# Delta stage of a fused decoder layer: squares for the gate's statistics in two halves, half of the sums after the copy of the states, and another order of two copies of the inverse

## The reference, cut to what matters

```python
q, k, v = silu(conv(x @ Wq)), silu(conv(x @ Wk)), silu(conv(x @ Wv)); beta = sigmoid(x @ Wb)
# delta rule by chunks, per head (4 heads of 64)
attn = where(strict, -(kb @ k.T), 0); T = inv(eye - attn); u = T @ v; w = T @ kb      # kb = k * beta
step: u_i = u0 - w_i @ S; o_i = q_i @ S + local @ u_i; S = S + k_i.T @ u_i
paths = stack([fir_s(v), fir_m(v), fir_l(v), o_delta, v])                             # 5 paths
stats = for each path and head: mean(t), mean(t*t), mean(|t|), sqrt(sum(t*t))
logits = gelu(concat(x, stats) @ gW1 + gb1) @ gW2 + gb2
probs = softmax(logits / tau) * (1 - sum(eps)) + eps
y = rmsnorm(sum_p probs_p * path_p) * norm_w @ Wo
```

## Time and profile before

| | us |
|---|---|
| median of 3 runs | 940.93 (940.04 to 941.74) |
| the profiled execution, its own time | 938.07 |
| its span in the profile | 936.2 |
| steps 1 to 9 of the delta stage in it | some 183 to 400 |

### The profile page before, as it was taken

One profiled execution on the slowest core, in us unless ns is written; L12 is line 12 of the kernel. 1 busy time (PEld: TensorE's weight loads), 2 busy tenths in 40 slices (PEclk: granted clock), 3 DMA queues, 4 the chain that ended last, 5 costly groups with the idle time before them and its releaser, 6 DMA issues.

```text
span 936.2 us, 17146 instructions
## 1 busy us (share of the span) xinstructions
PE 822.1 (88%) x6187; PEld 613.2 (65%) x6187; DVE 594.9 (64%) x1431; ACT 448.9 (48%) x831; POOL 350.7 (37%) x321
## 2 busy tenths in 40 slices
PE   6888879789988998898478898899979999999895
PEld 5676657667766666677345555556866777777774
DVE  5799979656888888877546677853552333333255
ACT  5677747455655665443046665565412322223221
POOL 9421210003455645632202246334531332222684
PEclk9899989878999999799678999999999999999998
DMA  5689849988959875546635455308031222221512
GB/s 176 198 241 299 248 127 253 341 198 189 250 178 247 255 215 148 171 137 219 225 131 170 159 184 179 127 25 268 26 98 41 63 68 57 70 57 46 157 63 68
DMA packets 160723, 149.18 MB, mean 159 GB/s; under 512 B 92289, under 2 KB 129217, under 8 KB 159361
## 3 DMA queue, kind: packets, MB, share of 16 engines
q1 hardware_dynamic: 157232, 138.72, 50.3%
q0 software_dynamic: 3408, 9.38, 2.7%
HBM read 86.90 MB, written 61.03 MB: 158 GB/s over the span
## 4 chain that ended last, share of the span: by engine, by line
PE 56%; DVE 12%; ACT 12%; POOL 8%; DMA 5%; issue 5%; SPq 1%; POOLq 0%; DVEq 0%; ACTq 0%
PE ps L2730 10%; PE ps L2745 5%; PE ps L665 4%; PE ps L2594 3%; PE ps L1397 3%; DMA queries<-q_pad 3%; POOL hank L344 2%; PE ps L422 2%; POOL kept L2877 2%; DVE big L1449 2%; PE ps L2607 2%; PE ps L2103 2%; PE ps L2216 2%; PE ps L1552 2%; PE ps L1405 2%
## 5 line engine op out<-in xcount | busy, mean ns | idle before, releaser
L2730 PE MATMUL ps<-wr,xbT 128*128 x312 | 100.6, 465 | 1.8 <-ACT xbT L2766 1.8
L2153 DVE TENSOR_REDUCE cmx<-ps 128x4 f32<-128x1024 f32 x64 | 77.4, 1219 | 37.6 <-PE ps L2103 36.0
L2192 ACT ACTIVATE cross_room<-ps 128x1024 f32<-128x1024 f32 x64 | 65.6, 1024 | 52.1 <-PE ps L2116 50.5
L2819 POOL DMA_INDIRECT y_dram<-yb,dest_row x39 | 37.3, 957 | 134.2 <-DVE dest_row L2795 129.7
L1365 POOL TENSOR_TENSOR st<-st,exponent 128x20 f32<-128x20 f32 x16 | 56.5, 3532 | 64.4 <-DVE st L1340 62.8
L2730 PEld LDWEIGHTS ps<-wr,xbT 128*128 128x128 f32 x312 | 59.4, 191 | 30.1 <-issue 3.5
L549 DVE SCALAR_TENSOR_TENSOR room<-room 128x256 f32<-128x256 f32 x144 | 58.3, 478 | 11.1 <-ACT room L498 11.1
L2804 DVE TENSOR_TENSOR cross_room<-cross_room,ps 128x352 f32<-128x352 f32 x39 | 20.3, 521 | 60.6 <-PE ps L2730 60.6
L2774 ACT ACTIVATE cross_room<-ps 128x352 f32<-128x352 f32 x39 | 18.1, 465 | 73.6 <-PE ps L2730 73.6
L2810 DVE TENSOR_SCALAR yb<-ps,weight 128x256 f32<-128x256 f32 x39 | 18.9, 484 | 50.8 <-PE ps L2745 50.8
L422 PE MATMUL ps<-room,weights 128*128 128x256 f32 x192 | 46.2, 392 | 3.6 <-DMA room<-in_conv_v 2.6
(11 more groups left out here) (355 smaller groups left out, 2210.3 us busy)
## 6 DMA issues: line engine op xcount, KB each, us to landing
xs_dram<-staged SPq DMA_DIRECT2D x17, 1040.0 KB, 6.5
room<-in_gW SPq DMA_DIRECT2D x8, 1280.0 KB, 8.2
tok_dram<-room SPq DMA_DIRECT2D x8, 768.0 KB, 7.1
fir_dram<-room SPq DMA_DIRECT2D x6, 1024.0 KB, 7.3
paths<-fir_dram SPq DMA_DIRECT2D x48, 128.0 KB, 3.6
keys<-k_pad SPq DMA_DIRECT2D x28, 196.0 KB
queries<-q_pad SPq DMA_DIRECT2D x28, 196.0 KB
xb<-xs_dram SPq DMA_DIRECT2D x39, 130.0 KB, 2.3
```

The costliest lines, as they stand in the source:

```text
L2153: V.tensor_reduce(mx[:, :, half, :, g].rearrange("p t c -> p c t"), ps[:, pair(h), :].rearrange("p c (t k) -> p c t k", t=TT), AX.X, ALU.m ...
L2192: S.activation(pT[g % 2][:, pair(h)].rearrange("p c k t -> p (c k t)"), ps[:, pair(1 - h), :].rearrange("p c n -> p (c n)"), ACT.Exp, scal ...
L2730: m = nc.tensor.matmul(ps[:, 2 * (j % 2) + half, 0:FF], xbT[j % 2][:, k, :], wr[:, bass.ds(e, 1), k, half, :].rearrange("p e n -> p (e n)" ...
L2819: G.indirect_dma_start(env.y2_dram, bass.IndirectOffsetOnAxis(ap=dest_row[:, j % NI:j % NI + 1], axis=0), yb[j % 4][:], None).then_inc(*y_ ...
```

## The change

The squares (ACT) are made by two instructions, one for each half of the tokens: the first in round 1, the second in round 2 behind the copy of u. Each waits only until the sums of the batch before have read its half. DVE sums the squares of half 0 in round 2 and moves the other three sums a round on: those of half 1 stand in round 3 behind the copy of the states, |t| of half 0 in round 4, |t| of half 1 in round 5, behind lT and ahead of the last five softmax steps. In the inverse, the last two copies (L1189) change places: the one out of PSUM bank 0 comes first, and PE's turn of k, which writes bank 0, waits for one copy fewer. The sums, the copies and their sizes are the same.

```diff
         def pe_invert(b):
...
-            pe.wait_ge(s.gw, 4 * b)
+            pe.wait_ge(s.gw, 4 * b - 1)
             turned(0, tok[i][:, :, 1]).then_inc(*s.k_turned.up())
...
         def dve_invert(b):
...
-            for h, bank in enumerate((3, 0)):
+            for h, bank in ((1, 0), (0, 3)):
...
         def act_statistics(b):
...
-            act.wait_ge(s.stat, 6 * (b - 1) + 3)
-            S.activation(sqs[:].rearrange("p n t d -> p (n t d)"), paths[i][:].rearrange("p n t d -> p (n t d)"),
-                         ACT.Square).then_inc(*s.sq.up())
-            yield
+            for t in range(TT):
+                act.wait_ge(s.stat, 6 * (b - 1) + 2 + t)
+                S.activation(sqs[:, :, t], paths[i][:, :, t], ACT.Square).then_inc(*s.sq.up())
+                yield
...
         def dve_statistics(b):
...
             stat(0, 0, paths[i])
             yield
-            dve.wait_ge(s.sq, b + 1)
+            dve.wait_ge(s.sq, 2 * b + 1)
             stat(1, 0, sqs)
+            yield
+            dve.wait_ge(s.sq, 2 * b + 2)
             stat(1, 1, sqs)
             stat(0, 1, paths[i])
             yield
             stat(2, 0, paths[i], apply_absolute_value=True)
             yield
             stat(2, 1, paths[i], apply_absolute_value=True)
             yield
```

## The result

| | before | after |
|---|---|---|
| median of the runs, us | 940.51 (10 runs, 932.17 to 945.38) | 947.11 (10 runs, 942.9 to 951.15) |
| ratio, 95% interval | | 1.0068 (1.004 to 1.0096) |
| the profiled execution, own time / span | 938.07 / 936.2 | 946.84 / 945.0 |

The change makes the kernel 0.68% slower, some 6.4 us. Lines of the gate have moved by two in the changed kernel (the products L1449 are L1451, L1493 is L1495, L1580 is L1582, POOL's sum L1510 is L1512) and the squares L1332 are L1333; L1053, L1183, L1189, L1313 and L1340 are the same.

What follows compares the result with a forecast made beforehand. Full steps were taken as bound by a ring of waits through DVE, ACT and PE. Steps 1 and 2 -4.0, step 3 +2.0, steps 4 to 7 +7.8, step 9 +1.5: +7.3 on 940.93, 948.2 us; range 939.8 to 951.5.

Steps and rivals of the forecast that it cites:

- rival (b): DVE and POOL taking turns costs only the nearest row's 0.7 us; steps 3 to 7 pay 1.1 each; 943.9 us; chance 0.14.
- (d): Faster: DVE wins the port for its three products in a row, steps 3 to 7; -5.0, 935.9 us; chance 0.16.
- (f): Square between the gelus needs two more ACT table loads of 1.28 us in steps 4 to 7; 958.5 us; chance 0.01.
- Rival (e): The later softmax alone costs time, DVE-POOL turns and clock unchanged; -0.5, 940.4 us; chance 0.12.
- Step 2, -4.0: Steps 1 and 2: earlier copy of the states and one copy fewer before k gain 4.0 us, bounds 3.0 and 4.2.
- The cap: Step 3 cannot turn k before its tokens land at 220.1, so at most 4.2 us are gained.
- Step 3, +2.0: Gate of step 3: softmax ends later and all of POOL's work meets DVE's products, +2.0 us.
- rival (c): PE's longer waits drop its clock to 1.2 GHz for 2 to 4 us in steps 5 to 7; +3, 951; chance 0.08.
- Full steps, 4 x 1.95: Steps 4 to 7 each lose 1.9 us on DVE and POOL plus 0.05 on ACT, +7.8 together.
- The order: Full steps: moved sum of \|t\| ends the softmax 1.48 us later, idle before L1183 covers part; +0.35 a step.
- the lock: Full steps: DVE's and POOL's products take turns on the shared port, whole instructions at a time; +1.55 us a step.
- the ring: Steps 5 to 8: the chain of waits through DVE, ACT and PE, holding the squares (2.23 us) but no sums.

Runs made afterwards that it cites:

- e6: The changed kernel, unchanged, profiled a second time; 941.89 us (one run).
- e8: The changed kernel with the last two copies of the inverse back in the old order; 945.13 us, ratio 1.0067 to the kernel before.
- e1: The changed kernel with batches 1 to 7 back to whole squares and old sum places, swap kept; 935.14 us, ratio 0.9964 to the kernel before.
- e7: The changed kernel with only the sum of squares of half 1 behind the copy of the states, softmax at its old place; 937.31 us, ratio 0.9964.
- e2: The changed kernel with batch 0 (step 2) as in the kernel before, swap kept; 949.2 us, ratio 1.0094 to the kernel before.
- e3: The kernel before with only the swap of the inverse's last two copies; 939.26 us, ratio 0.9955, resting on 7 of 12 runs.
- e9: The kernel before with SP issuing the next tokens and inverses ahead of the paths in steps 1 and 2; 944.46 us, ratio 1.0023.
- e12: The kernel before with only the squares made in halves, sums at their old places, no swap; 941.49 us, ratio 0.9971.
- e5: The kernel before, unchanged, profiled a second time; 934.33 us (one run).
- e4: The changed kernel with POOL's two products waiting for DVE's three; 945.39 us, ratio 1.0083 to the kernel before.
- e11: e7 with SP issuing the next tokens and inverses ahead of the paths in steps 1 and 2; 940.02 us, ratio 0.9963 to the kernel before.

## Why the prediction was right, and which terms were off

The direction, the place and the mechanism were right: forecast 948.2 us (+7.3), measured 947.11 beside 940.51 (+6.6), within the range. That the two numbers are so close is in part luck: the full steps lost 4.8 us and not 7.8, nearer to the 1.1 a step of rival (b) than to the 1.95 of the forecast, and by the profiles the start of cross moved by 4.4 and 6.1 us; what is missing up to 6.6 lies where single profiles scatter by several us. Rivals (d) and (f) fell: DVE lost its turn to POOL three times in every full step, and the second square ran between the gelus with no table load (L1333 at 309.90, L1428 at 311.07). Rival (e) fell with the products of 4.01.

- **Step 2, -4.0:** the mechanism was right, L1213 stands behind L1075 and the copy of the states comes 3.7 us sooner counted from the turn of k, as forecast. The swap gives 0.33 at each of two turns instead of 0.41. The gain to k in step 3 was 4.4 in the first pair of profiles, and 1.9 in the second, in which step 2 took 22.5 us before and 20.9 after. The cap is real, its place at 220.1 was lucky (220.22 in e6, but 219.06 in e8, 221.25 in e1, 223.55 in e7). Wrong was the clause that the change doesn't move SP: L1023 was issued at 211.03 in the first profile, 1.7 sooner, and anywhere up to 216.26 (e7) in the others, and it landed after 7.1 to 7.9 us, in e8 after 5.6. In the first profile and in e8 the cap was not reached.
- **Step 3, +2.0:** measured +2.3 and +3.3, but for another reason in part. The products went from 2.58 to 3.86, +1.3; the rest is the lower clock at the start of the step, +1.2 and +2.0 by the turns. Kernels with the old order in step 2 had it too (e2, e3, e9 and e12, above), so it isn't shown to be the change's. Over all profiles this stretch is 1.4 longer with the new order in step 3 than with the old one (27.3 against 25.9, six and eight profiles): the term was put at 2.0 and is some 1.4.
- **The clock in full steps (rival c):** it did fall now and then, ahead of step 5 in the changed kernel (0.50 at 272 to 276 us) but also in e5 (0.57), and ahead of step 6 in e6 (0.50 at 300 to 304), with a turn 0.4 to 0.6 longer; in e7 the turn was 1.3 longer, in e3 3.1, and in e8 three turns together 3.5. So the size that rival (c) gave, +3, occurs in single executions, with the old order of the sums (e3) as with the new (e8); that the change makes it more frequent isn't shown. In e3 and e7 it began with the tokens: in step 7 PE waited 2.22 and 1.83 us for them ahead of the turn of k, as it did for 0.6 to 1.2 us in e1, e4, e5, e11 and e12. So the cap that the forecast had in step 3 is near in full steps as well. The turn in e3:

```profile
335.46 1.11 PE L1053 MATMUL ps<-ident,kept 128*128 128x128 f32 x4 [2.22 <-DMA kept<-tok_dram]
```

- **Full steps, 4 x 1.95:** measured 4 x 1.2. The order: 0.16 instead of 0.35, because L1580 to L1183 had taken 8.20 us and takes 8.36. ACT: +0.09 instead of 0.05; e7 and e12, turns of 27.1 with products of 3.06, show the same 0.1 by itself. The term that was mis-sized is the lock: 0.95 instead of 1.55. The working gave each product its full 0.69 us after POOL had let go, and POOL its full time after DVE. The rows show 0.55 after POOL's end for DVE, and for POOL after DVE's end 0.91 and 1.12, where 1.06 and 1.27 are its own times: some 0.15 us of each instruction run beside the other engine's. From the start of DVE's first product, 0.33 us before POOL's first ends, that is 0.33 + 0.55 + 0.91 + 0.55 + 1.12 + 0.55 = 4.01; with full times the same sum is 4.7. The lower bound from the nearest row, 0.7, was nearer than the 1.55; the working should have used the 1.54 and 1.4 of that row as they stood.
- **The rule of exclusive use:** each engine's instruction waits for the other's to end, and in e4 three products with POOL away take 1.90. The Trainium skill, "SBUF — State Buffer", section "SBUF: two separate sides", says that the two engines' shared port pair is locked exclusively for a whole instruction. The trace agrees with the taking of turns and not with its length to the full: some 0.15 us of each instruction lie outside the turn.
- **The path of the ring:** the forecast put L1580 behind L1552 on the ring. Before, the chain ran past it, over PE and ACT to L1183. It was the 1.14 us ahead of L1183 that kept DVE's queue off the chain, as the forecast's own term for the order has it, and the moved sum put it there.
- **Step 9, +1.5:** +1.7 and, in the second pair, +0.1; over all profiles with the new order that stretch is 1.4 longer than over those with the old one (100.2 against 98.8 from L1493 of step 8 to cross, six and eight profiles).

By its own steps the sum would be -4.4 + 2.3 + 4.8 + 1.7 = +4.4 in the first pair, +6.1 in the second, and the interval of the ratio is +3.8 to +9.0. **Open** is the size of the early gain. Every profile with the old order in step 2 (before, e5, e2, e3, e9, e12) has the clock at 0.50 somewhere between 204 and 216 us, after PE's pause; it was back at some 216 in three of them (before, e5, e9) and at 228 or later in the others, and step 2 took 22.5 to 27.2 us. With the new order it is at 1.00 from 208 to 212 in every profile and falls later, between 212 and 224; step 2 then took 18.9 to 21.9 us (e1, e4, e6, e7, e8 and after). So two single profiles can differ by 1 to 8 us here, and the runs say only that e1 and e7, which keep the early gain without the loss, are 0.4% faster than before. e12, whose step 2 took 25.3 us in the profile, is 0.3% faster as well, so these runs can't tell the gain of the new order in step 2 from what the halves alone bring; why e12 gains was not found.

## What to carry to other kernels

When work is moved out of an early step that had room, read the same queue in the steps that repeat: there the moved 1.48 us used up 1.14 us of idle time, which had hidden the queue's own work and kept most of POOL's products away from DVE's. Where DVE and POOL both have two-input products out of SBUF as here, count both queues as one from the moment that releases both, with some 0.15 us off at each change of turn, and look for waits and PSUM copies of DVE under which POOL's work can run. A gain at the start of a pipeline goes on only until the next transfer that SP issues behind others. And where single executions scatter as step 2 does here, look at the median of all runs before a gain of 0.4% is believed: that of e3 isn't there in it.

## What the runs showed of the hardware beyond what was expected

A DVE product that waits for POOL ends 0.55 us after POOL's instruction, though it takes 0.69 alone, in each of the three cases shown. DVE's two copies out of PSUM (L1183) took 0.86 us together both with POOL's product running from 296.70 on (changed kernel, 296.54) and with POOL idle (e4, 298.44). TensorE's granted clock fell to 0.50 behind stretches with pauses of PE (it was busy 1.78 of 4 us at 204 to 208 in e12, 2.54 of 4 at 212 to 216 in e6), and by the means of the 4 us windows it stayed down for some 7 us in before and e5, 10 in e9, and 20 to 24 in e12, e2 and e3, at nearly the same order of work in step 2. The scatter of step 2, 22.5 to 27.2 us, is as large as anything that the early half of this change can gain.
